# Products of head weights on quarters of TensorE's array, and unread small matmuls in its first idle time

## The reference

```python
q, k, v = heads(Wq), heads(Wk), heads(Wv)          # X @ W.T, 16 heads of 64
qn = jnp.max(jnp.linalg.norm(q, axis=-1), axis=-1)[..., None, None]   # per batch and head; kn alike
q, k = q / qn, k / kn
kv = jnp.cumsum(k[..., :, None] * v[..., None, :], axis=2)
num = jnp.cumsum(v, axis=2) + jnp.einsum('bhnd,bhnde->bhne', q, kv)
den = jnp.arange(1, n + 1) + jnp.einsum('bhnd,bhnd->bhn', q, jnp.cumsum(k, axis=2))
attention = (num / den[..., None]) @ Wo.T + bo
...
probs = softmax(xn @ router_w)                      # 8 experts, the best 2, weights normalised
experts = sum over the 2 of weight * (silu(xn @ gate[e]) * (xn @ up[e])) @ down[e]   # F = 352
```

## Time and profile before

| | us |
|---|---|
| Median of 2 runs | 1610.57 (1609.27 to 1611.87) |
| Span of the profiled execution, first to last instruction | 1610.3 |
| TensorE busy with matmuls in it | 1463.3 (91%) |
| VectorE busy | 1180.1 (73%) |
| POOL busy | 911.2 (57%) |
| ScalarE busy | 876.2 (54%) |
| Mean granted clock of TensorE | 0.962 of full speed |

### The profile page before, as it was taken

One profiled execution on the slowest core, in us unless ns is written; L12 is line 12 of the kernel. 1 busy time (PEld: TensorE's weight loads), 2 busy tenths in 40 slices (PEclk: granted clock), 3 DMA queues, 4 the chain that ended last, 5 costly groups with the idle time before them and its releaser, 6 DMA issues.

```text
span 1610.3 us, 39161 instructions
## 1 busy us (share of the span) xinstructions
PE 1463.3 (91%) x9330; PEld 1317.9 (82%) x9332; DVE 1180.1 (73%) x3304; ACT 876.2 (54%) x2000; POOL 911.2 (57%) x1257
## 2 busy tenths in 40 slices
PE   2999975999999999999999999999998699999960
PEld 2999964888888888888888888888887699999960
DVE  7999997777777777777777777777777655555532
ACT  2999973555555555555555555555455444444430
POOL 3200016776776776776776776776676455555544
PEclk7999996999999999999999999999999899999985
DMA  9000000000000000000000000000000122222229
GB/s 289 19 0 0 0 1 14 12 11 8 11 11 8 11 11 8 11 11 8 11 11 8 11 11 8 11 11 8 10 11 7 42 63 62 61 63 62 59 65 291
DMA packets 72171, 53.44 MB, mean 33 GB/s; under 512 B 7840, under 2 KB 67360, under 8 KB 72096
## 3 DMA queue, kind: packets, MB, share of 16 engines
q1 hardware_dynamic: 54560, 28.95, 7.0%
q0 software_dynamic: 9216, 19.17, 3.4%
q10 hardware_dynamic: 8320, 4.19, 0.9%
HBM read 28.33 MB, written 23.96 MB: 32 GB/s over the span
## 4 chain that ended last, share of the span: by engine, by line
issue 31%; POOL 30%; PE 29%; POOLq 4%; DVE 3%; SPq 1%; DMA 1%; ACT 0%; DVEq 0%; ACTq 0%
POOL Al L414 11%; PE ybank L1248 6%; PE bank L1037 5%; PE bank L1039 5%; PE bank L1038 5%; POOL sorted_tokens L408 4%; POOL Ml L396 3%; POOL ysum L424 3%; PE ybank L1241 3%; POOL Mt L388 2%; POOL Mh L394 2%; SPq L331 1%; POOL xa L426 1%; PE ybank L1037 1%; PE ybank L1038 1%
## 5 line engine op out<-in xcount | busy, mean ns | idle before, releaser
L414 POOL TENSOR_TENSOR Al<-Am,Ah 128x512 fp32r<-128x512 f32 x256 | 329.4, 1287 | 177.7 <-ACT Ah L615 170.9
L615 ACT ACTIVATE Ah<-Am 128x512 fp32r<-128x512 f32 x256 | 161.5, 631 | 334.0 <-DVE Am L873 334.0
L1153 PE MATMUL ybank<-Wx,zf 128*128 128x129 f32 x2072 | 276.5, 276 | 4.8 <-ACT zf L620 4.8
L1153 PEld LDWEIGHTS ybank<-Wx,zf 128*128 128x128 f32 x2072 | 261.0, 191 | 22.3 <-issue 12.8
L866 DVE SCALAR_TENSOR_TENSOR ul<-bank,uh 128x512 fp32r<-128x512 f32 x256 | 174.0, 690 | 90.7 <-ACT uh L609 81.8
L898 DVE SCALAR_TENSOR_TENSOR acc<-ybank,rden,acc 128x128 f32<-128x128 f32 x780 | 217.7, 341 | 0.1
L504 POOL DMA_INDIRECT expert_rows<-yt,wdi x136 | 132.1, 972 | 142.0 <-ACT yt L687 121.5
L873 DVE TENSOR_TENSOR Am<-bank,causal 128x512 f32<-128x512 f32 x256 | 174.6, 682 | 23.1 <-PE bank L1039 23.1
L609 ACT ACTIVATE uh<-bank 128x512 fp32r<-128x512 f32 x256 | 148.7, 593 | 72.1 <-PE bank L1039 65.7
L786 DVE TENSOR_REDUCE ssq<-sq 128x448 f32 (+1 forms) x320 | 168.6, 573 | 7.6 <-ACT sq L557 5.8
L620 ACT ACTIVATE zf<-bank 128x512 f32<-128x512 f32 x258 | 151.7, 588 | 39.9 <-PE bank L1039 39.1
(11 more groups left out here) (225 smaller groups left out, 3906.2 us busy)
## 6 DMA issues: line engine op xcount, KB each, us to landing
xt<-sorted_tokens SPq DMA_DIRECT2D x137, 66.0 KB
er<-expert_rows SPq DMA_DIRECT2D x16, 512.0 KB, 8.5
xa<-in_L_attn_X SPq DMA_DIRECT2D x8, 512.0 KB, 7.3
out<-ot ACTq DMA_DIRECT2D x8, 512.0 KB, 7.1
expert_rows<-yt,wdi POOLq DMA_INDIRECT x136
sorted_tokens<-pay,sidx POOLq DMA_INDIRECT x128
gu<-in_L_ffn_gate_proj SPq DMA_DIRECT2D x1, 1408.0 KB
gu<-in_L_ffn_up_proj SPq DMA_DIRECT2D x1, 1408.0 KB
```

What stands on the lines that cost most here:

```text
L414: pool.tensor_tensor(Al[:, q], Am[:, q % 2], Ah[:, q], ALU.subtract).then_inc(e_Al, 1)
L615: act.activation(Ah[:, q], Am[:, q % 2], ACT.Copy).then_inc(e_Ah, 1)
L1153: last = pe.matmul(ybank[q % 2][:, i // 2, VE * (i % 2):VE * (i % 2) + VE], zf[:, q % 2, i, :], Wx[:, HQ * q + i, :], start=True, stop=True)
```

## The change

Three things change.

1. The products of `M` and `W` are made in pairs of groups. For each pair TensorE goes over four rows of heads; in each it issues four matmuls, one per quarter of the array: `parity` picks the 64 rows, `half` the 64 columns of the result's partitions. Before, a matmul had 64 rows and all 128 columns. The two heads of a row lie in one pair of banks; each bank takes two quarters, of different row halves and different column halves. TensorE signals once per pair, by 2.
2. ScalarE copies each of these banks in two halves of 64 partitions, since the two halves now belong to different heads. `o` is as before.
3. TensorE gets `part_trials()` between the setup transposes and the norms: small matmuls on zeros in two new tiles, into banks 4 to 7, whose results nobody reads. POOL clears the two tiles. There are 32 quarters of 64 moving columns, 32 of 65, then eight times three full fp32r matmuls of 256 columns and four quarters of 64, then eight of 64 rows by 128 columns, eight of 128 rows by 64 columns, and eight on one and the same quarter.

```diff
+        trial_r, trial_f = place("trial_r", [P, 2 * P], f32r), place("trial_f", [P, 2 * P])
...
-        def heads_of(n):
-
-            h0 = 8 * (n // 2) + n % 2
+        HALVES = [slice(0, DH), slice(DH, P)]
+
+        def heads_of(n, half):
+
+            h0 = 8 * (n // 2) + (n + half) % 2
             return slice(h0, h0 + 7, 2)
...
             pool.memset(dn[:, :, FT - 1, :], 0.0).then_inc(f_dz, 1)
+            pool.memset(trial_r[:].bitcast(f32), 0.0).then_inc(s_trial, 1)
+            pool.memset(trial_f[:], 0.0).then_inc(s_trial, 1)
...
                     dst = WoT[:, 4 * n:4 * n + 4, :]
+                    act.activation(dst, bank[j % 4][:].rearrange("p (h d) -> p h d", d=D), ACT.Copy).then_inc(s_lateh, 1)
                 else:
-                    dst = Mf[:, heads_of(n), :] if kind == "M" else Wx[:, heads_of(n), 0:D]
-                act.activation(dst, bank[j % 4][:].rearrange("p (h d) -> p h d", d=D), ACT.Copy).then_inc(s_lateh, 1)
+                    for half in range(2):
+                        c = HALVES[half]
+                        dst = Mf[c, heads_of(n, half), :] if kind == "M" else Wx[c, heads_of(n, half), 0:D]
+                        last = act.activation(dst, bank[j % 4][c, :].rearrange("p (h d) -> p h d", d=D), ACT.Copy)
+                    last.then_inc(s_lateh, 1)
...
+            def quarter(n, width):
+
+                r, c = slice(64 * (n % 2), 64 * (n % 2) + 64), slice(64 * (n // 2 % 2), 64 * (n // 2 % 2) + 64)
+                o = 65 * (n // 4 % 4)
+                pe.matmul(bank[4 + n % 2][c, o:o + width], trial_f[r, c], trial_f[r, 0:width], start=True, stop=True)
+
+            def part_trials():
+
+                pe.wait_ge(s_trial, 2)
+                for n in range(32):
+                    quarter(n, 64)
+                for n in range(32):
+                    quarter(n, 65)
+                for n in range(8):
+                    for m in range(3):
+                        pe.matmul(bank[6][:, 0:2 * P], trial_r[:, 0:P], trial_r[:], start=True, stop=True)
+                    for m in range(4):
+                        quarter(m, 64)
+                for n in range(8):
+                    r = slice(64 * (n % 2), 64 * (n % 2) + 64)
+                    pe.matmul(bank[6 + n % 2][:, 0:P], trial_f[r, 0:P], trial_f[r, 0:P], start=True, stop=True)
+                for n in range(8):
+                    c = slice(64 * (n % 2), 64 * (n % 2) + 64)
+                    pe.matmul(bank[6][c, 0:65], trial_f[:, c], trial_f[:, 0:65], start=True, stop=True)
+                for n in range(8):
+                    quarter(0, 64)
+
+            part_trials()
...
-                dst = bank[j % 4]
                 if kind == "o":
-                    last = transpose4(dst, "o", n)
-                else:
+                    transpose4(bank[j % 4], "o", n).then_inc(s_late, 1)
+                elif n % 2 == 1:
                     if kind == "W":
                         pe.wait_ge(s_lateh, 6)
                     left, right = (wqn, wkn) if kind == "M" else (wvn, WoT)
                     for i in range(4):
-                        h = heads_of(n).start + 2 * i
-                        r = slice(DH * (h % 2), DH * (h % 2) + DH)
-                        last = pe.matmul(dst[:, P * i:P * i + P], left[r, h // 2, :], right[r, h // 2, :], start=True, stop=True)
-                last.then_inc(s_late, 1)
+                        for parity in range(2):
+                            for half in range(2):
+                                r, c = HALVES[parity], HALVES[half]
+                                dst = bank[(j - 1 + (parity ^ half)) % 4][c, P * i:P * i + P]
+                                last = pe.matmul(dst, left[r, 4 * (n // 2) + i, c], right[r, 4 * (n // 2) + i, :],
+                                                 start=True, stop=True)
+                    last.then_inc(s_late, 2)
```

More of the change, by code:

```diff
@@ L195, in build @@
         s_stat, s_chain, s_rt, s_sqrt = sem("s_stat"), sem("s_chain"), sem("s_rt"), sem("s_sqrt")
-        s_rw = sem("s_rw")
+        s_rw, s_trial = sem("s_rw"), sem("s_trial")
         n_xn, n_xT, n_xTh, n_xTl = sem("n_xn"), sem("n_xT"), sem("n_xTh"), sem("n_xTl")
```

## The result

The changed kernel took 1624.32 us (median of 2 runs, 1623.07 to 1625.56) against 1610.57. The ratio is 1.0086, with a 95% interval of 1.0056 to 1.0115. So it is slower by 0.9%, by less than 2%, but clear of noise; the forecast of 1611.5 (1606.8 to 1619.0) missed it. The profiled execution has a span of 1623.8 us.

What follows compares the result with a forecast made beforehand. VectorE was taken to set the pace of the norms and the late stage, with TensorE not waited for. Trial overrun, clock gain and late stage summed as 1610.3 + 2.7 - 1.5 + 0 = 1611.5 us, range 1606.8 to 1619.

Steps and rivals of the forecast that it cites:

- the length of the code: Over 500 more instructions ahead of the norms: fetching them by DMA was costed at 0.
- The bound of 4 us: Upper limit on the cost of fetching the longer code, with DMA engines full from 18 to 33 us.
- the overrun of 2.7 us: Trial matmuls ahead of the norms end at 36.0 us instead of 33.31, delaying everything behind by 2.7 us.
- the 1.5 us of clock: Trials hold TensorE at 2.4 GHz into the norms' first products, saving 1.5 us (bounds 0 and 2.0).
- The pair rate of 0.069 us as a floor: Each weight load and matmul pair, in trials and quarter products, takes 0.069 us on TensorE.
- Rival (a): Four quarters at once, pairs at 0.028 us or less, trials end before 33.3 us: 1608.8 us; chance 0.27.
- Changes of array form: In the trials, 21 changes of array form on TensorE at 0.09 us each, 1.9 us together.
- The late stage at cost 0: Quarter products for `Mf` and `Wx` and ScalarE's doubled copies stay hidden behind the chain of waits: cost 0.
- Rival (b): Quarters run one after the other, `Mf` takes 7.1 us, late-stage scatters 4.8 us later: 1616.3 us; chance 0.15.
- Rival (c): Trials run serially at 1.2 GHz: 1629 us; or code-fetch stalls there: 1615 to 1629; chance 0.13 together.

Runs made afterwards that it cites:

- Run 3: The changed kernel plus eight more trial quarters (32 instructions) in the same idle time; 1610.17 us, ratio 0.9997 to the kernel before.
- run 4: The kernel before plus 35 unread full-array matmuls and one transpose (142 instructions) in TensorE's first idle time, no quarters; 1623.8 us, ratio 1.0083.
- run 7: The changed kernel plus 28 unread full fp32 matmuls behind the trials, filling the idle time up to the norms; 1608.61 us, ratio 0.9988 to the kernel before.
- run 2: The changed kernel without the trial matmuls and their two memsets, so quarters and half copies alone; 1619.3 us, ratio 1.0058 to the kernel before.

## Why the prediction was wrong

- **The step that failed** is the one on the length of the code: "I cost that at 0, because TensorE is busy 963 of 995 us in the attention stage". That row shows that straight code is fetched in time. It says nothing of a jump back, and the timeline of the kernel before had the sign of it, a gap of 0.67 to 0.91 us on "issue" at each of the three jumps, to which the prediction gave no row. The bound of 4 us, set for a fetch under full DMA engines ahead of the norms, was also put in the wrong place: the norms start at 33.30 us as before, and the fetches at the jumps cost 13. Runs 3 and 4 settle it from both sides: 32 more instructions undo the loss, 142 in the old kernel make it. Run 3 also shows what the forecast would have been worth without this step: 1610.17 us lies near 1611.5, but by luck, since neither the overrun of 2.7 us nor the 1.5 us of clock was there.
- **The pair rate of 0.069 us as a floor** fell. It was how two row halves overlap when each comes in a group of eight, not how fast TensorE is fed: with the row half changing at each matmul they start each 0.059 us, quarters each 0.015, the products' records each (1.98 - 0.27) / 63 = 0.027. Rival (a) had the rate right, 0.028 and half of that; the forecast overrun of 2.7 us did not exist. The Trainium skill ("TensorE: Matmul & The Clock Gate", section "Measured speedup vs the span model"), which that rival named, adds about 4 ns for each further tile. In this trace a further quarter record comes 0.015 us after the one before, a quarter of the 0.06 that one alone takes, so it doesn't show the 4 ns. The total of rival (a), 1608.8, was wrong all the same, by the loss at the jumps and by the clock, next.
- **The clock's gift of 1.5 us** was sized right (1.3 to 1.5 us in run 7, which started 0.3 late) and granted wrongly. It hung on the overrun: with the trials over at 26.3 us, the clock had fallen before the norms. I had carried the same term over to rival (a), where the trials end early, without asking what 7 us of idle time do; the earlier trace rows had shown the clock at 0.50 from 18.2 us after TensorE stopped at 14.9.
- **Changes of array form** were undercounted at 0.09 us: one round of three full matmuls and four quarters takes 0.82 us (in the trace from 16.81 to 17.63 us), of which 3 x 0.107 and 8 x 0.015 are 0.44, so 0.19 for each of the two changes. The trials ended early in spite of it, because the quarters were so cheap.
- **The late stage at cost 0** held: the first scatter is at 252.38 for 252.44. The copies took 0.607 instead of 0.565 us, half the partitions saving nothing, as costed. `ra` ended at 232.35 instead of 233.5, since the first banks were ready earlier.
- **Rival (b)** is refuted by the 64 records in 1.98 us. **Rival (c)** named a range of loss that the result falls into, 1615 to 1629 with fetch stalls, but by luck: it put them at the trials, through which the clock held and which ended early.

## What to carry to other kernels

Instructions that cost nothing where they stand still shift the code behind them. Ahead of a long loop count them: where its body started 40 instructions of TensorE or fewer before the end of a 16 KB block of code, each jump back stood a second time, and behind stalls of 2.35 us and more the clock fell as well; with 60 instructions, some 3 us of work here, nothing was lost. No view names the place of a block's end; the second stall does. Before a slowdown in an untouched loop is explained by the edit, add a few unread instructions ahead of it and see whether it goes; and look at each jump back of the old kernel for gaps on "issue".

## What the runs showed of the hardware

- Stalls of 1.59 to 1.90 us left the clock at 1.00 (run 2 at all three jumps), stalls of 2.35 to 2.63 us with 0.60 to 1.00 us of gap ahead of them brought it to 0.50 for 3.2 to 6.7 us (the changed kernel and run 4 at all three). From the first jump's matmul to the second's, run 2 takes 1.79 us more than the kernel before with a stall of 1.59 (753.44 - 509.34 against 242.31), the changed kernel 4.25 with one of 2.63. So 1 us more of stall cost some 2.4 us more.
- In the late stage quarters that differ in row half and column half ran together with two of them writing one bank of PSUM: 64 fp32 records in 1.98 us, 0.027 each. With four at once a full stream of 128 columns at 0.111 would give 0.028, so nothing was halved. The Trainium skill ("TensorEngine Tiling (Array Packing)", section "Gotcha 1: PSUM Pressure") says that different row tiles cannot access one bank at the same time, which taken as taking turns would have halved that rate; this trace does not agree. The trials say nothing of it: there the two quarters that share a bank have the same row half.
- On one quarter alone a record of 64 columns starts each 0.06 us, on four quarters in turn each 0.015 (the trials).
- Full matmuls on zeros kept the clock at 1.00 through 7 us, up to the norms (run 7), with an output that nobody reads.
